# Graph network, late adjacency products: two products of the same chunk as one product of 384 columns

## The reference

```python
edge_index = jnp.stack([src, dst])
h = relu(layernorm(x))
# layer 0
msg_input  = concat([h[src], edge_attr])            # E x 128
messages   = relu(msg_input @ W1 + b1) @ W2 + b2    # E x 64
aggregated = segment_sum(messages, dst, N)
x = x + (relu(concat([h, aggregated]) @ U1 + c1) @ U2 + c2)
# layer 1
h = relu(layernorm(x))
x = x + segment_sum(h[src] * edge_weight[:, None], dst, N)
```

## Time and profile before

| | |
|---|---|
| time, median of 3 runs | 3185.72 us (3183.37 to 3192.08) |
| the profiled execution's own time | 3187.68 us, span 3185.9 us |
| granted PE clock, mean | 0.815 of full speed |
| PE busy | 2226.9 us (70% of the span) |
| PEld busy | 1783.8 us (56%) |
| DVE busy | 1623.8 us (51%) |
| ACT busy | 846.2 us (27%) |
| POOL busy | 1560.2 us (49%) |
| DMA | 459.65 MB, mean 144 GB/s |

### The profile page before, as it was taken

The page is one execution under the profiler, slowest core; times in us unless marked ns, Lnnn a source line. Parts: engine busy times, 40 slices in busy tenths (PEclk is TensorE's granted clock), DMA queues, the critical chain, the costliest instruction groups (busy, mean ns, idle before and its releaser), DMA issues.

```text
span 3185.9 us, 52358 instructions
## 1 busy us (share of the span) xinstructions
PE 2226.9 (70%) x19560; PEld 1783.8 (56%) x19560; DVE 1623.8 (51%) x4964; ACT 846.2 (27%) x1500; POOL 1560.2 (49%) x1635
## 2 busy tenths in 40 slices
PE   4465756656666677677677777777777767677699
PEld 3354545544554555555556665665656655556587
DVE  4444755555454545544454455545545544444455
ACT  4122432322222223322222222222222222122221
POOL 4735255555555555554555455555555544444400
PEclk9977877777787787777778778877988888778899
DMA  4123535334633463355245534543554355425588
GB/s 87 35 91 133 188 106 171 135 127 138 194 126 113 139 195 114 115 166 179 93 128 173 169 95 148 169 143 110 180 155 139 102 156 174 135 83 158 155 269 288
DMA packets 376809, 459.65 MB, mean 144 GB/s; under 512 B 78474, under 2 KB 298890, under 8 KB 372968
## 3 DMA queue, kind: packets, MB, share of 16 engines
q1 hardware_dynamic: 317914, 401.54, 38.8%
q0 software_dynamic: 51712, 53.06, 6.9%
q10 hardware_dynamic: 6926, 1.63, 0.2%
HBM read 281.50 MB, written 174.54 MB: 143 GB/s over the span
## 4 chain that ended last, share of the span: by engine, by line
PE 51%; another core or an unknown queue 17%; issue 16%; DVE 12%; ACT 3%; DMA 1%; DVEq 0%; ACTq 0%; SPq 0%
PE pair L1292 18%; PE pair L1307 8%; PE pair L1325 7%; PE pair L1232 5%; PE pair L1279 4%; DVE bld L1799 4%; DVE bld L1809 3%; ACT stage L998 2%; PE pair L1225 2%; PE pair L1427 2%; PE pair L1330 1%; DVE rings L1753 1%; PE pair L1357 1%; DVE bld L1802 1%
## 5 line engine op out<-in xcount | busy, mean ns | idle before, releaser
L824 POOL DMA_INDIRECT rows<-table,idx x1464 | 1398.8, 955 | 1316.8 <-DVE rings L1753 920.7
L1292 PE MATMUL pair<-bld 128*128 128x300 bf16 x4848 | 869.1, 334 | 251.2 <-ACT stage L998 156.5
L998 ACT COPY stage<-pair 128x600 f32<-128x600 f32 x808 | 524.8, 665 | 1834.0 <-remote 859.9
L1799 DVE TENSOR_SCALAR bld<-iota_key,key 128x300 bf16<-128x300 f16 x1616 | 529.5, 328 | 849.8 <-remote 470.2
L1292 PEld LDWEIGHTS pair<-bld 128*128 128x128 bf16 x4848 | 563.4, 123 | 487.1 <-issue 241.0
L1809 DVE TENSOR_TENSOR bld<-bld,part 128x512 bf16<-128x512 bf16 x1212 | 492.7, 407 | 0.0
L1307 PE MATMUL pair<-stage,h 125*64 125x96 f32 x4230 | 350.0, 308 | 98.3 <-issue 97.7
L1232 PE MATMUL pair<-w1b,rings 128*128 128x128 f32 x1584 | 260.5, 317 | 172.5 <-DVE rings L1753 171.0
L1307 PEld LDWEIGHTS pair<-stage,h 125*64 125x64 f32 x4230 | 291.0, 179 | 122.5 <-issue 121.8
L1232 PEld LDWEIGHTS pair<-w1b,rings 128*128 128x128 f32 x1584 | 239.0, 228 | 191.9 <-DVE rings L1753 186.0
L1279 PE MATMUL pair<-hot,rings 128*64 128x40 f32 x3232 | 195.1, 244 | 211.9 <-issue 137.2
(11 more groups left out here) (178 smaller groups left out, 1496.8 us busy)
## 6 DMA issues: line engine op xcount, KB each, us to landing
late_piece<-adjacency SPq DMA_DIRECT2D x232, 480.0 KB
rings<-in_edge_attr_dram SPq DMA_DIRECT2D x202, 256.0 KB
adjacency<-stage SPq DMA_DIRECT2D x14, 2160.0 KB
tail<-stage SPq DMA_DIRECT2D x101, 240.0 KB
stage<-tail SPq DMA_DIRECT2D x50, 480.0 KB, 5.7
rows<-table,idx POOLq DMA_INDIRECT x1464
adjacency<-stage SPq DMA_DIRECT2D x10, 1920.0 KB
adjacency<-stage SPq DMA_DIRECT2D x10, 1680.0 KB
```

What stands on the lines that cost most here:

```text
L824: pool.indirect_dma_start(out=to[:, t, :], out_offset=None, in_=table, in_offset=bass.IndirectOffsetOnAxis(ap=idx[:, g, t:t + 1], axis=0), ...
L998: act.copy(tiles[:, g % STAGE, :, 2 * j * WT:2 * (j + 1) * WT].rearrange("p h (o w) -> p o h w", w=WT), build_pair[i % 2][:, :, 0:KEYS].re ...
L1292: last = pe.matmul(build_pair[i // 2 % 2][:, t % 2, 0:KEYS], hot_w[q % 2][k][:, :, u], hot_key[q % 2][:, u, :], start=(k == 0), stop=(k == ...
L1799: return dve.tensor_scalar(hot_key[q % 2][:, u, :], iota_key[:, :], key[:, g, t + u:t + u + 1], None, ALU.is_equal)
```

## The change

`late_products` now asks whether exactly two products are left to make here and both are of the same chunk (`late_joined`). If so, both are made together: each matmul reads its columns from both slots of `late_piece` and writes 384 columns of `mid_bank` (L1325), or 2 x 96 (L1330). PE waits for both pieces before the first matmul, and `late_done` rises by two after the last. The place of each product in `mid_bank` follows its slot (`late_place`), so that the first of a pair may lie in the second half. The planner gets a `continue`: where the next two products are of one chunk and the second isn't due yet, the step makes none.

```diff
--- before.py
+++ after.py
@@ -172,6 +172,9 @@
         until = min([at for at in READY if at > s] + [GROUPS])
         due = sum(READY[c] <= s and QUAD * q + QUAD + 3 <= s for c, q in waiting)
         upto = 3 if due > 2 * sum(not updating(i) for i in range(s, until)) else 2
+        if len(waiting) > 1 and s < GROUPS - 2 and waiting[0][0] == waiting[1][0] and \
+                s < max(READY[waiting[1][0]], QUAD * waiting[1][1] + QUAD + 3):
+            continue
         while waiting and len(LATE_AT[s]) < upto:
             c, q = waiting[0]
             if s < max(READY[c], QUAD * q + QUAD + 3):
@@ -186,9 +189,17 @@
 
     LATE_QUAD = [q for s in range(GROUPS) for _, _, q in LATE_AT[s]]
 
+    def late_joined(s, first, upto):
+
+        return upto - first == 2 and LATE_AT[s][first][1] == LATE_AT[s][first + 1][1]
+
     def late_place(s, i):
 
-        return max(i - 1, 0) if len(LATE_AT[s]) == 3 else i
+        many = len(LATE_AT[s])
+        first = 1 if many == 3 else 0
+        if i >= first and late_joined(s, first, many):
+            return LATE_AT[s][i][0] % LATE
+        return max(i - first, 0)
 
     def late_by(s):
 
@@ -1311,7 +1322,8 @@
 
             def late_products(s, first, upto):
 
-                for i in range(first, upto):
+                joined = late_joined(s, first, upto)
+                for i in range(first, upto, 2 if joined else 1):
                     n, c, q = LATE_AT[s][i]
                     if i == first:
                         wait_count(pe, late_kept, n)
@@ -1319,18 +1331,25 @@
                         wait_count(pe, acc_added, s if len(LATE_AT[s]) == 3 and first == 0 else s + 1)
                     pe.wait_ge(h2_staged, c + 1)
                     pe.wait_ge(late_loaded[n % LATE], 16 * (n // LATE + 1))
-                    held = late_piece[0:NP, n % LATE, :].rearrange("p (g h c) -> p g h c", g=QUAD, c=GC)
-                    at = late_place(s, i) * QCOLS
+                    if joined:
+                        pe.wait_ge(late_loaded[(n + 1) % LATE], 16 * ((n + 1) // LATE + 1))
+                        held = late_piece[0:NP, :, :].rearrange("p s (g h c) -> p (s g) h c", g=QUAD, c=GC)
+                        at, many = 0, 2
+                    else:
+                        held = late_piece[0:NP, n % LATE, :].rearrange("p (g h c) -> p g h c", g=QUAD, c=GC)
+                        at, many = late_place(s, i) * QCOLS, 1
                     for h in range(BLK - 1):
-                        pe.matmul(half_of(mid_bank, h)[:, at:at + QCOLS],
+                        pe.matmul(half_of(mid_bank, h)[:, at:at + many * QCOLS],
                                   h2[:, (c * BLK + h) * D:(c * BLK + h + 1) * D], held[:, :, h, :],
                                   start=(h < 2), stop=False)
 
-                    for i in range(2):
-                        last = pe.matmul(half_of(mid_bank, i)[:, at + i * COLS:at + (i + 1) * COLS],
+                    for k in range(2):
+                        to = half_of(mid_bank, k)[:, at:at + many * QCOLS].rearrange("p (s c) -> p s c", s=many)
+                        of = held.rearrange("p (s g) h c -> p s g h c", s=many)
+                        last = pe.matmul(to[:, :, k * COLS:(k + 1) * COLS],
                                          h2[:, (c * BLK + BLK - 1) * D:(c + 1) * BLK * D],
-                                         held[:, 2 * i:2 * i + 2, BLK - 1, :], start=False, stop=True)
-                    last.then_inc(late_done, 1)
+                                         of[:, :, 2 * k:2 * k + 2, BLK - 1, :], start=False, stop=True)
+                    last.then_inc(late_done, many)
 
             def late_apart(s):
                 if len(LATE_AT.get(s, [])) == 3:
```

## The result

The changed kernel takes 3125.85 us (median of four runs, 3122.63 to 3136.84) where the kernel before takes 3184.55 (3176.08 to 3192.08): ratio 0.983, 95% interval 0.9803 to 0.9857. That is 59 us less. The forecast was 131 us less, so the direction was right and the size was over twice too large; the measured time is next to that of rival B (3122), though not for B's reason. The profiled execution of the changed kernel has a span of 3120.8 us against 3185.9.

The account below looks back on a forecast made before the run. The prediction took the hold on PE's completions behind the gathers as the bound. Savings of 91 (two-product steps), 37 (long steps) and 3 (ordinary three-product steps), 131 us, took 3187.7 to 3056.7; 2.0 lower for the median, rounded to 3055 us, range 3010 to 3165.

Parts of the forecast that it names:

- rival B: Two-product and long steps: the fourth pair is seen somewhat earlier but the quad still ends late; 64 us, 3122; chance 0.13.
- What bounds the kernel: Whole step: the loop of eight gathers, late release of PE's completions, L1787, L1753, pre_made; 13.0 to 14.8 us a step.
- the hold: Second half of a gather batch: PE's completions reach other engines late, until about 1.5 to 2 us after the last gather.
- PE's time or its number of instructions: Ahead of the fourth pair: the number of PE instructions decides; same PE time, 24 against 48, periods 13.2 against 14.8.
- Two-product steps, 91 us: 66 ordinary two-product steps: a joined step nears a one-product step's period, 1.38 us saved each; 91 us (49 to 119).
- line of records: In the gather batch: PE completions are passed on at a fixed rate per instruction, 4.2 per us.
- Long steps, 37 us: Three-product stretches and two-product steps before an update: 15, 11 and 11 us saved, 37 us (0 to 45).
- Added wait and moved late_done: Pair's wait for both pieces and late_done's later rise: cost nothing in two-product steps, covered by some 8 us.
- rival C: Three-product steps and the late-freed slot: the pair's wait makes the kernel slower, 3228 at most, 3207 half hidden; chance 0.08.
- A: Two-product steps: nothing moves, the period stays 14.83 as it follows columns or the gathers alone; 3185; chance 0.11.
- The rule that the prediction sets beside A: Late matmuls: each costs its columns over the clock plus about 2.5 ns, so 1224 fewer records are worth 3 us.
- D: The hold: an effect of the recording, so an execution without records might neither have it nor gain; kept within A.

Follow-up runs that it names:

- half_gathers: The kernel before with four of the eight gathers of each group left out from the 22nd group on: 2210.93 us, ratio 0.7033.
- joined_split_2: The changed kernel with a pair's waits and late_done kept but each product in its own matmuls, 48 records a pair: 0.9991 of the kernel before.
- narrow_before: The kernel before with three quarters of the columns of most late matmuls left out, every instruction kept: ratio 0.9987.
- narrow_joined: The changed kernel with three quarters of the columns of most late matmuls left out, every instruction kept: 0.9665 of the kernel before.
- before_2: The kernel before, unchanged, run and profiled again on one chip with variants of the change: ratio 1.0007.
- q_behind_2: The changed kernel with make_q moved from between the second and third pair of tiles to behind the fourth: 0.961 of the kernel before.

## Why the prediction was wrong in size

**What bounds the kernel.** Right, on the chip that was profiled: the hold behind the gathers, told from the period of L1787 and not from busy time. half_gathers bears it out. What I could not see from one trace is that the hold isn't there on every chip.

**PE's time or its number of instructions.** The prediction took the number alone, from one comparison of a one-product and a two-product step. It is number and time. joined_split_2 (0.9991 against 0.9838) shows that the change gains by the fewer instructions. Of the two things that these bring, n falls by 20 and the pair ends 0.8 us earlier; the earlier end alone gains nothing, as narrow_before has it at 6.1 us with n = 93 and 0.9987. narrow_joined (0.9665) shows that the time of the joined product, which doesn't shrink, keeps the gain small, though its cut also took n from 86 to 74.

**Two-product steps, 91 us: the step that failed.** The forecast was 1.38 us for each of the 66 ordinary ones; the median gave 0.10, and all of them together some 13 us. "If it behaves as the one-product step" was the sentence, and three things were wrong in it. First, the time at which the fourth pair was seen in the kernel before (2315.20) is the release, a cap, and not a point on the line of records. With n = 106 nearly every pair is held to that cap (153 of 153 in the last column of the table of steps); taking 20 records off moved nothing that could show in most steps. I had written that 24 records are worth 5.7 us of which only 1.84 can be used, as if the 5.7 began at the cap. The rate of 4.2 per us has the same fault: its later point is the release too. And the pairs that are seen before the release don't lie on a line of records: in the kernel before, the 70th record of the step at 735.4 is seen 9.98 us behind the first gather and the 82nd of the step at 577.4 at 10.02 us. Second, a joined step is no one-product step: n is 86 against 82, because less of the longer matmuls has ended when the first gather comes, and the pair ends at 6.7 to 6.9 us instead of 4.8 to 5.9. Third, there are only three one-product steps, and they lie on the edge: 13.2, 13.2 and 14.0 in the kernel before, and in before_2, the same kernel, 14.7, 14.7 and 13.2. Two of the latter:

```profile
L1787 DVE TENSOR_TENSOR nodes<-nodes,pair x2: 186/188/189, 578.4 to 593.1; 128x40 f32 x2
...
L1787 DVE TENSOR_TENSOR nodes<-nodes,pair x2: 190/194/198, 1850.3 to 1863.6; 128x40 f32 x2
```

**Long steps, 37 us.** Right in place and size: 16.5, 11.6 and 10.3 us against 15, 11 and 11, and joined_split_2, with 48 records again, has the steps of 20 us back (166.4 us for the ten). The reason that the earlier trace rows gave, a second product whose late_done falls into the hold, is only in part confirmed: such waits remain, as the row of L1848 shows, without a long step. Some 7 us more came from single long two-product steps that the prediction left out by counting only 66 of 77. The size is partly luck, as the number of long steps varies from run to run: in before_2 the same ten take 173.7 us.

**Added wait and moved late_done.** Nothing to be seen on the chips with the hold, as costed: joined_split_2, which has both and no saving, is at 0.9991, with 15.7 us of waiting for pieces in the trace of the change. On the chips without it, rival C's side: +0.3%.

**Rivals.** A is refuted by joined_split_2: the same columns and waits without the fewer records gain nothing. The rule that the prediction sets beside A (The Trainium skill, TensorE: Matmul & The Clock Gate, section Back-to-back issue gap), by which the fewer matmul records are worth an estimated 3 us, fits neither kind of chip: 47 to 59 us were gained with the hold, and 7 us lost without. B has the number, 3122, by luck: it wanted 49 us from ordinary two-product steps and 15 from long ones, and it was some 13 and 45. D stays open, and the prediction dismissed it too fast. It argued from the other runs taking as long as the profiled one, but each of them has a span and a granted clock beside its time, so none is known to have run without records. That the hold goes with the number of records would fit D as well. On chips 14 and 9 the same records are made without a hold, so records alone don't make it; whether it is there on the other chips when nothing is recorded, no run shows.

## What to carry to other kernels

Where an event is seen at a release, its measured time is a cap and says nothing about how far behind the cap it would otherwise lie: before pricing what is taken away ahead of it, work out the distance first, here n against the n of steps that are seen early. An equal count is not an equal step; check the stand-in in as many steps as there are, and if there are three and they differ, give them the width that they have. Run a kernel on more than one chip before tuning it to a wait that the profile can't name: moving `make_q` was worth 2.3% on one, and the change that gained 1.6% there cost 0.3% on the other. And where a price follows the number of records, time the kernel once with the recording off before you tune to it; that is what is missing here.

## What the runs showed of the hardware that was not expected

The same kernel takes 2230 us on two chips (medians of 2232.59 and 2229.63, chips 14 and 9) and 3141 to 3186 on the others (medians of four groups of runs, chips 2, 4 and 8 and that of the result). No numbered chip was used on two occasions, so these runs don't separate the chip from the occasion. Where it is slow, PE's completions arrive late in the batches of gathers (762 of 1747 by more than 0.9 us) and those still held come together, 1.5 us behind the end of the last gather in the earlier trace rows and 1.7 in the earlier trace rows; where it is fast, 15 of 1740. The gathers themselves are issued at the same 1.25 us on both. What makes the difference was not found, and whether the hold is there when nothing is recorded is open.

PE's own issue seems to be held too: late in a batch two small matmuls start 0.72 us apart (2334.91 and 2335.63 in the trace of the change). And direct work left over by a short step makes short and long steps alternate when a kernel is near the edge (q_behind_2: 13.3, 14.9, 13.3, 14.7 us).
